# A decoder layer on one core: the cross-attention's query weight multiplied into the context's keys once, in place of a queries stage for each batch element

## The reference

```python
xn = layernorm(x)                                    # per element b: 256 x 256
Q = (xn @ W_Q).reshape(b, -1, 16, 64)                # 256 x 1024
K = (ctx @ W_K).reshape(b, -1, 16, 64)               # 77 x 1024
scores = einsum('bhqd,bhkd->bhqk', Q, K) / 8         # masked entries -> -1e9, then softmax over 77
```

## Time and profile before

| | us |
|---|---|
| median of 3 runs (lowest, highest) | 631.1 (630.52, 634.54) |
| the profiled execution | 631.86 |
| its span, first to last instruction | 630.1 |
| TensorE busy in the span | 525.6 |
| VectorE, ScalarE, POOL busy | 397.1, 288.5, 192.1 |

### The profile page before, as it was taken

One profiled execution on the slowest core, in us unless ns is written; L12 is line 12 of the kernel. 1 busy time (PEld: TensorE's weight loads), 2 busy tenths in 40 slices (PEclk: granted clock), 3 DMA queues, 4 the chain that ended last, 5 costly groups with the idle time before them and its releaser, 6 DMA issues.

```text
span 630.1 us, 12060 instructions
## 1 busy us (share of the span) xinstructions
PE 525.6 (83%) x4576; PEld 445.2 (71%) x4576; DVE 397.1 (63%) x1107; ACT 288.5 (46%) x440; POOL 192.1 (30%) x285
## 2 busy tenths in 40 slices
PE   0697767888767799799879997999798979999986
PEld 0695536766755687598759975997587758888776
DVE  3757476982681489547964797379734973677642
ACT  3262241336354334563457335833582457264634
POOL 3525181155224142414232413332330224021310
PEclk9799687789997799899989998999999998999999
DMA  7685382113304103310232013400340020000000
GB/s 250 228 225 162 139 259 57 38 68 83 79 1 135 51 20 104 95 47 19 69 107 71 19 21 124 101 19 3 111 116 19 2 60 1 19 22 22 1 17 18
DMA packets 47129, 47.28 MB, mean 75 GB/s; under 512 B 14640, under 2 KB 42944, under 8 KB 47072
## 3 DMA queue, kind: packets, MB, share of 16 engines
q1 hardware_dynamic: 45568, 41.57, 23.2%
q0 software_dynamic: 1504, 4.95, 2.2%
HBM read 30.71 MB, written 15.53 MB: 73 GB/s over the span
## 4 chain that ended last, share of the span: by engine, by line
PE 68%; DVE 11%; ACT 9%; POOL 6%; issue 4%; DMA 1%; SPq 0%; DVEq 0%; POOLq 0%; ACTq 0%
PE banks L680 13%; PE banks L682 12%; PE banks L681 12%; PE banks L990 5%; PE banks L932 5%; PE banks L943 4%; PE banks L836 3%; PE banks L823 3%; PE banks L802 2%; DVE banks L1799 2%; ACT probs L1369 2%; POOL probs L556 2%; ACT work L1336 2%; PE banks L880 2%; DVE sm L1885 1%
## 5 line engine op out<-in xcount | busy, mean ns | idle before, releaser
L1799 DVE CUSTOM_DVE_ANT_0 banks<-banks,causal_qk 128x256 f32<-128x256 f32 (+1 forms) x256 | 83.9, 386 | 8.4 <-PE banks L802 7.4
L556 POOL TENSOR_SCALAR_AFFINE_SELECT probs<-probs 128x256 f32<-128x256 f32 x128 | 52.3, 438 | 98.2 <-ACT probs L1369 98.0
L545 POOL TENSOR_TENSOR work<-work,rc 128x616 f32<-128x616 f32 x32 | 39.0, 1218 | 124.0 <-DVE rc L1887 124.0
L1369 ACT ACTIVATE probs<-banks 128x768 f32<-128x768 f32 x64 | 50.3, 812 | 46.2 <-PE banks L823 40.6
L1336 ACT ACTIVATE work<-banks 128x1024 f32<-128x1024 f32 x28 | 28.7, 1026 | 56.1 <-PE banks L932 56.1
L680 PE MATMUL banks<-k_hi,q_hi 128*128 128x256 f32 (+1 forms) x144 | 47.6, 331 | 5.5 <-DVE k_lo L1659 5.5
L680 PE MATMUL banks<-wo_hi,c_hi 128*128 128x256 f32 x128 | 38.6, 302 | 7.7 <-DVE c_lo L1752 7.7
L802 PE MATMUL banks<-k_stack,q_stack 62*128 62x256 f32 (+1 forms) x256 | 29.9, 312 | 16.5 <-DVE mneg L1799 14.9
L802 PEld LDWEIGHTS banks<-k_stack,q_stack 62*128 62x128 f32 x256 | 20.4, 195 | 31.1 <-issue 14.5
L681 PE MATMUL banks<-k_lo,q_hi 128*128 128x256 f32 (+1 forms) x144 | 42.2, 293 | 0.0
L682 PE MATMUL banks<-k_hi,q_lo 128*128 128x256 f32 (+1 forms) x144 | 42.2, 293 | 0.0
(11 more groups left out here) (211 smaller groups left out, 1658.9 us busy)
## 6 DMA issues: line engine op xcount, KB each, us to landing
rot_dram<-rot_s_hi SPq DMA_DIRECT2D x16, 256.0 KB, 3.1
rot_dram<-rot_s_lo SPq DMA_DIRECT2D x16, 256.0 KB, 3.3
q_stack<-rot_dram SPq DMA_DIRECT2D x32, 128.0 KB, 2.8
k_stack<-rot_dram SPq DMA_DIRECT2D x32, 128.0 KB, 3.1
k_raw<-k_dram SPq DMA_DIRECT2D x16, 154.0 KB, 3.3
v<-v_dram SPq DMA_DIRECT2D x8, 308.0 KB
x_in<-in_x SPq DMA_DIRECT2D x8, 256.0 KB, 3.2
x<-in_x SPq DMA_DIRECT2D x8, 256.0 KB, 4.4
```

The source lines that it names most:

```text
L545: pool.tensor_tensor(sc2[g % 2], sc2[g % 2], rc2[:, g % 2].rearrange("p g a -> p g a ()").broadcast_to([P, 4, 2, S2]), ALU.mult).then_inc( ...
L556: last = pool.affine_select(out=diagonal, in_=diagonal, compare_op=ALU.is_ge, fill=0.0, base=0, pattern=[[0, 2], [1, P]], channel_multipli ...
L1369: act.activation(probs[:, n:n + 2, :], bank[:, bk:bk + 2, P:4 * P], ACT.Exp, scale=SCALE).then_inc(p_ok, 1)
L1799: last = dve.tensor_tensor_reduce(out=scores_q, in0=scores_q, in1=causal_qk[:, 1 - q:2].rearrange("p a n -> p (a n)"), scale=-1.0, scalar= ...
```

## The change

- A new stage `fold(m, k)` multiplies, for all elements at once, the query weight of a pair of heads (m), half of its 256 input features (k), with the pair's keys: for each half of 308 columns three products, each as two matmuls of 64 rows, one head each. W_Q is passed transposed. ScalarE empties k = 0 and VectorE k = 1, in an order by element and head, to one of three slots of 1232 columns; SyncE stores each slot (`store_folded`, 0.63 MB) to `ck_dram`. A slot is used again when its store has landed. `keys(m)` now leaves a high and a low part on chip, in two alternating buffers.
- `queries` goes, on all engines. `scores2(b, g)` multiplies the normalised, transposed x (`xbT`) with the folded keys of four heads, 308 columns, two halves of the features and three products each.
- `context(b)` loads 1.26 MB in four DMAs in place of 0.31 MB in two. `context_keys(b, g)` is split in four groups: ScalarE copies, POOL subtracts (VectorE before).
- The query weight now lies where W_O of the cross-attention comes later; that weight is loaded after the last fold and its low part is made by POOL.
- All lists are in a new order. In `first`, keys and folds are interleaved with attention 0, the values' products lie behind it, and the scores of element 1 precede element 0's cross-attention. In `step`, TensorE's and SyncE's lists change as below; VectorE's list loses its queries and key parts, takes `mask_bias` first and `statistics_b` of the next element after the third hidden group.

```diff
+        fold_slots = [raws["ck"][:, j * 2 * NS:(j + 1) * 2 * NS] for j in range(2)] + [work[:, 4 * NS:6 * NS]]
...
+            def store_folded(m, k):
+                i = KD * m + k
+                sp.wait_ge(fold_ok[k], 2 * m + 2)
+                sp.dma_start(ck_dram[:, k, m].rearrange("p b n -> p (b n)"), fold_slots[i % FS]).then_inc(fold_st[i % FS], 16)
...
+                if last_element(b):
+                    sp.wait_ge(st_ps, HH * NB)
+                    sp.sem_inc(waited_sp, 1)
+                    sp.wait_ge(rot_st, 16 * 4 * NB)
+                else:
+                    sp.wait_ge(s2_ps, 4 * b)
                 sp.sem_inc(waited_sp, 1)
-                for p in range(2):
-                    sp.dma_start(
-                        own_keys(raws["k2"])[p],
-                        k2_dram[64 * p:64 * p + DX].rearrange("p m (b s) -> p m b s", s=S2)[:, :, b, :]
-                    ).then_inc(k2_ld, 16)
+                for h in range(2):
+                    pairs = slice(h * XM // 2, (h + 1) * XM // 2)
+                    for k in range(KD):
+                        sp.dma_start(raw_half(b, k, h).rearrange("p (m n) -> p m n", n=PAIR),
+                                     ck_dram[:, k, pairs, b]).then_inc(ck_ld[h], 16)
...
+            def context_keys(b, g):
+                pool.wait_ge(ck_hi, 4 * b + g + 1)
+                for k in range(KD):
+                    raw = raw_half(b, k, g // 2)[:, g % 2 * QUAD:(g % 2 + 1) * QUAD]
+                    last = pool.tensor_tensor(ck_low(b, k, g), raw, ck_high(b, k, g).bitcast(F32), ALU.subtract)
+                last.then_inc(ck_lo, 1)
...
+                    pe.wait_ge(fold_ok[0], 2 * m - 1)
+                at = 3 + 2 * ((5 * m - 2) % 2) if m else 3
                 for half in range(2):
-                    n = 2 * m + half
-                    if n >= 4:
-                        pe.wait_ge(kx_ok, n - 3)
                     for k in range(KD):
-                        mm = product(bank[:, 3 + n % 4, 0:HS], both(wk2, slice(None), k, slice(m * P, m * P + P)),
+                        mm = product(bank[:, at + half, 0:HS], both(wk2, slice(None), k, slice(m * P, m * P + P)),
                                      both(ctx_s, slice(None), k, slice(half * HS, (half + 1) * HS)),
                                      k == 0, k == KD - 1)
-                    mm.then_inc(kx_ps, 1)
+                mm.then_inc(kx_ps, 1)
+            def fold(m, k):
+                if m == 0 and k == 0:
+                    pe.wait_ge(w_lo[WQ_W], 1)
+                if k == 0:
+                    pe.wait_ge(kx_hi, m + 1)
+                    pe.wait_ge(kx_lo, m + 1)
+                for half in range(2):
+                    if k == 0:
+                        if m > 0:
+                            pe.wait_ge(fold_ok[1], 2 * m - 1 + half)
+                        at = 3 + 2 * ((5 * m + 1 + half) % 2)
+                    else:
+                        if half == 0:
+                            pe.wait_ge(fold_ok[0], 2 * m + 2)
+                        elif m + 1 < XM:
+                            pe.wait_ge(kx_hi, m + 2)
+                            pe.wait_ge(kx_lo, m + 2)
+                        at = 3 + 2 * ((5 * m + 4 + half) % 2)
+                    for first_, last_, i, j in ((True, False, 0, 0), (False, False, 0, 1), (False, True, 1, 0)):
+                        for p in range(2):
+                            rows = slice(64 * p, 64 * p + DX)
+                            mm = pe.matmul(bank[:, at + p, 0:HS], wq2[i][rows, m, k * P:(k + 1) * P],
+                                           kT[m % 2][j][rows, half * HS:(half + 1) * HS], start=first_, stop=last_,
+                                           skip_group_check=True)
+                    mm.then_inc(fold_ps, 1)
...
-            def queries(b, g):
+            def scores2(b, g):
+                pe.wait_ge(ck_hi, 4 * b + g + 1)
+                pe.wait_ge(ck_lo, 4 * b + g + 1)
                 if g == 0:
                     pe.wait_ge(xbT_hi, norm_index(b, 0) + 1)
                     pe.wait_ge(xbT_lo, norm_index(b, 0) + 1)
-                    if b == 0:
-                        pe.wait_ge(w_lo[WQ_W], 1)
-                    elif not last_element(b):
+                    pe.wait_ge(mask_ok, b + 1)
+                    if not last_element(b):
                         pe.wait_ge(gl_ok, 4 * b)
-                elif g == 3 and last_element(b):
-                    pe.wait_ge(q2_lo, 4 * b + 1)
-                for c in range(2):
-                    m = 2 * g + c
-                    for k in range(KD):
-                        mm = product(halves(queries_bank(b, g))[:, c, :], both(wq2, slice(None), k, slice(m * P, (m + 1) * P)),
-                                     both(normed(b), slice(None), k), k == 0, k == KD - 1)
-                mm.then_inc(q2_ps, 1)
-            def scores2(b, g):
-                if g == 0:
-                    pe.wait_ge(q2_lo, 4 * b + (3 if last_element(b) else 2))
-                    pe.wait_ge(mask_ok, b + 1)
-                    pe.wait_ge(k2_lo, 2 * b + 2)
                 else:
                     pe.wait_ge(sub_ok, 4 * b + g)
-                for c in range(2):
-                    m = 2 * g + c
-                    dst = halves(scores2_bank(b) + c)
-                    for q in range(QT):
-                        pe.matmul(dst[:, q, 0:PAIR], ident_bf[:], mask_bf[:, q].rearrange("p a s -> p (a s)"),
-                                  start=(q == 0), stop=False, skip_group_check=True)
-                    for q in range(QT):
-                        mm = product(dst[:, q, :], both(cross_queries(b), slice(None), m, slice(q * P, (q + 1) * P)),
-                                     both(k2, slice(None), slice(m * PAIR, m * PAIR + W)), False, q == QT - 1,
-                                     skip_group_check=True)
+                at = scores2_bank(b)
+                for q in range(QT):
+                    pe.matmul(bank[:, at + q, 0:QUAD], ident_bf[:], mask_bf[:, q].rearrange("p a s -> p (a s)"),
+                              start=True, stop=False)
+                for q in range(QT):
+                    for k in range(KD):
+                        mm = product(bank[:, at + q, 0:QUAD], both(normed(b), slice(None), k, slice(q * P, (q + 1) * P)),
+                                     (ck_high(b, k, g), ck_low(b, k, g)), False, k == KD - 1)
                 mm.then_inc(s2_ps, 1)
...
                     rotated = n + 1 if N else a + 1
-                transpose_b(b, 0)
                 if N:
                     project(n, 0)
-                queries(b, 0)
-                queries(b, 1)
+                transpose_b(b, 0)
                 if N:
                     project(n, 1)
                 scores2(b, 0)
-                queries(b, 2)
                 if A:
                     scores(a, 0, rotated)
-                queries(b, 3)
+                scores2(b, 1)
                 if A:
                     scores(a, 1, rotated)
-                scores2(b, 1)
+                    scores(a, 2, rotated)
                 transpose2(b, 0)
-                if A:
-                    scores(a, 2, rotated)
+                scores2(b, 2)
+                if A:
+                    scores(a, 3, rotated)
                 weigh2(b, 0)
-                if A:
-                    scores(a, 3, rotated)
-                scores2(b, 2)
+                scores2(b, 3)
+                if A:
+                    scores(a, 4, rotated)
                 transpose2(b, 1)
-                if A:
-                    scores(a, 4, rotated)
                 output2(b, 0)
+                if A:
+                    scores(a, 5, rotated)
                 weigh2(b, 1)
                 if A:
-                    scores(a, 5, rotated)
-                scores2(b, 3)
+                    scores(a, 6, rotated)
                 transpose2(b, 2)
                 output2(b, 1)
                 if A:
-                    scores(a, 6, rotated)
+                    scores(a, 7, rotated)
                 weigh2(b, 2)
                 if A:
-                    scores(a, 7, rotated)
+                    transpose_max(a)
                 transpose2(b, 3)
                 output2(b, 2)
-                if A:
-                    transpose_max(a)
                 weigh2(b, 3)
+                if A:
+                    shifted(a, 0)
                 output2(b, 3)
...
                     shifted(a, 4)
+                    weigh(a, 0)
+                    shifted(a, 5)
                 transpose_b(b, 1)
                 if A:
-                    weigh(a, 0)
+                    shifted(a, 6)
                     weigh(a, 1)
-                    shifted(a, 5)
                 narrow(b)
                 if A:
-                    shifted(a, 6)
                     shifted(a, 7)
...
             def keys(m):
-                for half in range(2):
-                    n = 2 * m + half
-                    act.wait_ge(kx_ps, n + 1)
```

(70 more changed lines are left out.)

797 lines of the change are left out of this document (409 added, 388 removed).

## The result

The changed kernel takes 628.6 us (median of 20 runs, 623.6 to 633.4) beside 631.8 us for the kernel before (20 runs): a ratio of 0.993, 95% interval 0.991 to 0.995. So it is 3 us faster where I forecast 26, and outside my range. The profiled execution took 626.4 us, with a span of 624.7.

A forecast was written before the change was run, and what follows sets the result against it. TensorE was taken to bound two thirds of a step and VectorE its middle. Five steps -20, drain -5 and fill -1 us sum to -26, so 605 us, forecast range 595 to 615 (0.60), wider range 590 to 623.

The forecast's parts named there:

- Together 4.4 us: In each step: 1.9 us won at the last context group plus 2.5 later, before 0.5 off for ScalarE's queue.
- so I cost it at nothing; its cover is POOL's idle time: In each step: POOL's new key subtractions, about 7 us an element, cost nothing; without cover one group, 1.7 us, late.
- VectorE's queue is late there too: In each step: reason for charging only 0.5 of 0 to 1.7 us for key copies in ScalarE's queue.
- sets the pace: In each step: VectorE, with 22 us of softmax and maxima, paces the second transposes of probabilities, which gain only 0.7 us.
- The 0.5 us for ScalarE's queue: In each step: two key-copy groups ahead of a probabilities copy and a context copy cost 0.5 us, bounds 0 to 1.7.
- The fill: Up to the first result: 14 us more TensorE work against 59.9 us idle; forecast -1 us, bounds -12 to +20.
- That is off the path, unless it delays the first normalisation: In the fill: POOL taking over the split of the output weight costs nothing, barring a delayed first normalisation.
- Rival A: In the fill: folds wait for evacuations and maxima, so their 19 us lie bare; +12 to +20, total 618 to 626; chance 0.15.
- The term of 19 us: In the fill: 96 pairs of fold matmuls at 0.20 us each on TensorE, 19 us, bounds 13.5 to 27.
- Rival C: In the fill: the stores' DMA rate makes the kernel slower, total 640 to 660 us; chance 0.05.
- B: Whole kernel: the fill gains too, fill -9, steps -4.6, drain -7, total 590 to 593 us; chance 0.13.
- D: VectorE's stretch and ScalarE's queue hold steps at 63.5 us or more, fill takes the drain's gain; 624 to 634; chance 0.07.

The follow-up runs named there:

- fill_covers: Changed kernel with output-weight split on VectorE, POOL's first key group behind the causal masks, 68 unread matmuls in fill and drain, none in steps: 613.3 us, 0.970 of the kernel before.
- pool_keys: Changed kernel, but in each step POOL splits the next element's first key group behind the last causal mask: 627.4 us, 0.993 of the kernel before.
- again: The changed kernel itself, unedited, run as the base for the other runs: 630.1 us, 0.997 of the kernel before.
- half_covered: best_cover with half of the maxima of elements 3 to 7 left out: 612.6 us, 0.968 of the kernel before.
- half_maxima: Changed kernel, but elements 3 to 7 take maxima only over the second half of the queries: 628.2 us, 0.988 of the kernel before.
- scalar_keys: Changed kernel, but ScalarE makes each step's third key group behind the fifth exponential and second copy of transposes: 629.7 us, 0.996 of the kernel before.
- pool_vector: Changed kernel with the cross output weight split on VectorE and POOL's first key group behind the causal masks: 624.4 us, 0.988 of the kernel before.
- vector_split: Changed kernel, but the cross output weight is split on VectorE behind element 0's transposed copies, not on POOL: 626.6 us, 0.990 of the kernel before.
- best_cover: Changed kernel with output-weight split on VectorE, POOL's first key group behind the causal masks, 68 unread matmuls in fill and drain, 15 a step: 614.3 us, 0.971 of the kernel before.
- fold_third: Changed kernel, but the fold makes one of three product terms, 64 of 192 matmuls: 630.2 us, 0.997 of the kernel before.
- small_stores: Changed kernel, but each folded-key store writes only the first element's eighth and all elements load those keys: 627.9 us, 0.993 of the kernel before.
- before_fill_covers: The kernel before the change with 59 unread matmuls of 512 columns in the waits of its fill: 624.0 us, 0.988 of the kernel before.

## Why the prediction was wrong, step by step

**The step.** TensorE's saving was right: 58.82 less 52.52 is 6.3 us, 1.7 of it the slow stretch, so 4.6 where I said 4.8; a cross-score group takes 2.07 us (2.04 forecast). The step of 60.5 came out near for what I had costed, 60.9 without POOL's hold, and the steps of fill_covers sum to 303.5 us, 19 less than before, where I said 20. But that is luck: in fill_covers no step has a slow stretch, in the kernel before each has one, and at 1.45 us each they are 7 of the 19. At like clock a middle step wins 2.5 us (64.9 less 1.45, against 60.9) and not 4.0, for TensorE idles 8.4 us in it (60.93 less 52.51) where it idled 6.1. The sum "Together 4.4 us" failed here: it took nearly all of the saved work as time. With the queries gone TensorE waits 1.9 us a step for the softmax of the group before (1.44 of it in the row at 360.42 above), which the kernel before had covered; I saw that bare latency in the drain and not in the step. This is read from the two traces; no run put other work there alone.

The second thing that failed is "so I cost it at nothing; its cover is POOL's idle time". POOL had the time, but its new instructions hold VectorE's: 0.7 us at the maxima in each step, shown by pool_keys. My bounds asked only how late POOL would be, not whom it would stop. That is 3.5 of the 7.7 us missing. Some 1.5 more is the fourth step with its slow stretch (62.95 against 61.4 in `again`), and 2.3 the first step (64.0 against 61.7, and 63.2 against 60.9 in fill_covers), which I took as equal to the others. It holds a leftover of the fill, the output projection of element 2's self-attention, 12 matmuls more than in the next step and a wait of its own:

```profile
227.41 0.36 PE L729 MATMUL banks<-wo_hi,attn_hi 128*128 128x256 f32 x1 [1.07 <-DVE attn_lo L1843]
```

**"VectorE's queue is late there too", "sets the pace".** Wrong: half_covered and half_maxima. TensorE does wait for VectorE's results, but making VectorE's stretch shorter wins next to nothing; I read a saturated engine as the bound. The 0.5 us for ScalarE's queue was an overcharge (scalar_keys), and loads cost nothing, as taken; the only wait of ScalarE for them is 0.3 us in the drain. (The upper rate of 300 GB/s that I named for them stands in neither of the rows I gave, which reach 259.)

**The fill.** Forecast -1, measured +9. Attention 0 was transposed at 88.6, as I had said (90). But the low part of element 0's last context group starts at 171.6, where my hand schedule had that group at 161 and the kernel before has it at 158.2: the values' products stand between, from 99.5 to 117.2, then waits for the maxima of attention 1 of 1 to 1.8 us a group, then the hold. From there to the first result it takes 55.6 us, before 60.0. "That is off the path, unless it delays the first normalisation" was the step that failed; I named the condition and gave it no price. It was 4 us of a held instruction, on the path (TensorE idle for 5.61 us). Moving it to VectorE gave back 3.4 us by the medians (626.6 against 630.1; 3.0 in pool_vector against pool_keys), but as few as 0.1 and 1.7 where it stayed on POOL, so these 3 us are not clear of the spread; first results in single profiles (227.2 and 229.5 for the changed kernel, 227.3 for vector_split) don't settle it. With covers in both, the first result stands at 217.9 (best_cover, 8.5 us of clock lost until then) to 223.6 (half_covered, 20.5) against 210.8 (6.8): 7 us late at about like clock. The fill has some 9 us of TensorE work more (13.8 less 4.8), but fold_third took 9 us of it out and won nothing, at a lower clock. Rival A, +12 to +20, was nearer than my -1 but too large. TensorE waited 2.1 us for evacuations between folds and 4.8 us for the low parts of the keys, and small_stores shows no cost of the stores. I cannot say how much is the fold and how much the order of values and scores, as no run moved the values back; most of the fill's loss stays open. The term of 19 us was mis-sized: 13.8. The Trainium skill's rule on tiles of different row groups ("TensorE: Matmul & The Clock Gate", "Part 3: Packing small matmuls") had given this side of my bounds.

**Rival C** is excluded: 8.8 MB less stored, nothing clear won, and the DMA ran at 232 GB/s from 28.5 to 60 us and 264 from 60 to 110, about as forecast. **B** failed in all three parts: +9, -2.5 a step and -2 where it had -9, -4.6 and -7. **D** had the total (624 to 634) and named a fill that takes gains back, but its steps of 63.5 were wrong (62.1).

**The drain**: -5 forecast, -2.1 measured, at the end of its bounds (-2 to -9); 2.1 us of clock are lost in it, before 0.4.

**The clock** had no term in the sum. In the kernel before the steps lose 1.7 us each to it, in the profile after two of five do. The change's gain of 12.3 us in the steps thus holds some 5 us of clock, and its runs spread over 10 us with it. At covered fills on both sides the mended change is worth 0.970 / 0.988, 1.8%, 10.7 us (fill_covers has 15 covers in its drain too, and some 6 us of this is the slow stretches of four steps that only before_fill_covers has).

## What to carry to other kernels

Work moved to an idle POOL is not free: ask which VectorE instructions stand beside it, and price each at up to the full length of POOL's. A TensorE timeline with small gaps has a second price, the granted clock: list the stretches at 1.2 GHz before and after, and compare steps of the same clock before you explain a few us. A saturated engine in a stretch is a suspect like a busy share is: take some of its work away and see. Work that is removed may have covered a latency: ask what TensorE does in its place.
